# Computing one of four cross-attention score products three times in every unit

## What is computed

```python
q = (x @ Wq + bq).reshape(1, B * N, H, hd)
kv = (cond @ Wkv + bkv).reshape(1, -1, 2, H, hd)
q, k, v = _fq_sym(q, -1), _fq_sym(k, -1), _fq_sym(v, 2)
attn = softmax(einsum('bhqd,bhkd->bhqk', q, k))
attn = _fq_unsigned(attn, axis=-1)
out = einsum('bhqk,bhkd->bhqd', attn, v)
```

## Time and profile before

| | us |
|---|---|
| median of three runs (2273.24 to 2276.38) | 2275.49 |
| the profiled execution | 2284.15 |
| its span, first to last instruction | 2282.2 |
| attention within the span, 1206 to 2078 | 872 |
| TensorE busy over the span | 1910.6 (84%) |
| VectorE busy over the span | 1695.9 (74%) |
| ScalarE busy over the span | 1592.8 (70%) |

### The profile page before, as it was taken

One profiled execution on the slowest core, in us unless ns is written; L12 is line 12 of the kernel. 1 busy time (PEld: TensorE's weight loads), 2 busy tenths in 40 slices (PEclk: granted clock), 3 DMA queues, 4 the chain that ended last, 5 costly groups with the idle time before them and its releaser, 6 DMA issues. The chain is left out here.

```text
span 2282.2 us, 40123 instructions
## 1 busy us (share of the span) xinstructions
PE 1910.6 (84%) x12006; PEld 1240.5 (54%) x12006; DVE 1695.9 (74%) x2836; ACT 1592.8 (70%) x2475; POOL 525.3 (23%) x430
## 2 busy tenths in 40 slices
PE   6988999999999999997877777777777777775999
PEld 5776877777777878786552222222222222222787
DVE  5885676777777776768877888888888888885433
ACT  4667888888888888887377777777777777774211
POOL 2002555555555555554000000000000000002001
PEclk8998999999999999999895555555555555555999
DMA  4000000000000000000106888878888878886000
GB/s 131 15 5 28 0 28 0 28 0 28 0 28 0 28 12 16 28 0 25 36 1 120 156 153 153 156 150 153 154 152 153 155 151 153 155 158 143 10 10 19
DMA packets 557870, 164.78 MB, mean 72 GB/s; under 512 B 535040, under 2 KB 550272, under 8 KB 557824
## 3 DMA queue, kind: packets, MB, share of 16 engines
q1 hardware_dynamic: 557824, 164.18, 35.4%
HBM read 27.83 MB, written 2.10 MB: 13 GB/s over the span
## 5 line engine op out<-in xcount | busy, mean ns | idle before, releaser
L1247 ACT ACTIVATE levels<-s_ps,nb,qstep 128x1024 int16<-128x1024 f32 x512 | 612.2, 1199 | 235.9 <-DVE nb L1187 235.9
L1176 DVE TENSOR_REDUCE mx<-s_ps 128x1 f32<-128x512 f32 (+1 forms) x768 | 661.3, 868 | 93.6 <-PE s_ps L1122 85.6
L1122 PE MATMUL s_ps<-kT,qT 48*128 48x512 bf16 x1024 | 521.1, 611 | 233.5 <-ACT levels L1247 232.0
L602 DVE SCALAR_TENSOR_TENSOR xs<-x_ps,cw,xs 128x508 f32<-128x508 f32 (+2 forms) x393 | 291.4, 741 | 174.2 <-ACT xs L524 135.8
L1122 PEld LDWEIGHTS s_ps<-kT,qT 48*128 (+1 forms) x1024 | 82.2, 103 | 483.0 <-issue 460.9
L493 PE MATMUL o_ps<-wo,hid 128*128 x1024 | 242.9, 380 | 5.0 <-DVE acc L589 5.0
L658 POOL TENSOR_TENSOR hid<-y,sg 128x512 f32<-128x512 f32 x128 | 175.5, 1371 | 277.5 <-ACT sg L546 184.8
L1132 PEld LDWEIGHTS ao_ps<-vi,levels_T 128*128 128x128 f16 x4096 | 129.3, 105 | 185.5 <-issue 185.5
L1472 POOL MEMSET minus_half_o<- 128x4 f32 x1 | 0.1, 103 | 998.6 <-POOLq L1065 998.6
L493 PEld LDWEIGHTS o_ps<-wo,hid 128*128 128x128 f32 x1024 | 192.7, 189 | 39.5 <-issue 9.9
L524 ACT ACTIVATE xs<-x_ps,cb,cw 128x512 f32<-128x512 f32 x131 | 101.9, 777 | 116.2 <-PE x_ps L445 116.1
(11 more groups left out here) (196 smaller groups left out, 3244.8 us busy)
## 6 DMA issues: line engine op xcount, KB each, us to landing
w_raw<-winT_dram SPq DMA_DIRECT2D x18, 512.0 KB, 4.5
wo_raw<-woutT_dram SPq DMA_DIRECT2D x9, 512.0 KB, 5.8
levels_T<-levels SPq DMA_TRANSPOSE x256, 4.3
acc<-xT_dram SPq DMA_DIRECT2D x4, 512.0 KB, 6.1
w_bc<-winT_dram SPq DMA_DIRECT2D x16, 128.0 KB, 2.3
acc<-x_dram SPq DMA_DIRECT2D x1, 2048.0 KB, 11.2
att<-ctxT_dram SPq DMA_DIRECT2D x4, 512.0 KB, 6.0
out_dram<-f_out SPq DMA_DIRECT2D x16, 128.0 KB, 1.7
```

The lines of the kernel that those rows point to most:

```text
L602: dve.scalar_tensor_tensor(to, x_ps[:, :, 0:SEQ - s], cw[:, head, TAPS - 1 - s], to, ALU.mult, ALU.add).then_inc(chain if s < TAPS - 1 els ...
L1122: return pe.matmul(s_ps[:, BANKS[h % 2][chunk], :], qT[0:PARTS * HD, bass.ds(round_, 1), h % NH, :].rearrange("p b t -> p (b t)"), kT[:, h ...
L1176: dve.tensor_reduce(mx[:, h % 2, at:at + 1], src, AX.XY if what == "cd" else AX.X, ALU.max).then_inc(max_done, 1)
L1247: act.activation(levels[:, s, half * HALF:(half + 1) * HALF].rearrange("p (c k) -> p c k", c=2), s_ps[:, first:first + 2, :], ACT.Exp, bia ...
```

## The change

In `body` of TensorE, the product b of unit n+2 is issued three times instead of once. All three read the same keys and queries, write the same bank with the same values, and each starts a new sum (`start=True, stop=True`), so the scores are the same. Only the third increments `b_ready`. Nothing changes in the operands: keys and queries keep 48 rows. The products that stand ahead of the loop (units 0 and 1) stay single. So two more matmuls run in every unit but the last two, 508 in all, each with its own weight load.

```diff
                     if exists(qt, h, 2):
+                        for _ in range(2):
+                            score(qt, h + 2, "b")
                         score(qt, h + 2, "b").then_inc(b_ready, 1)
```

## The result

The changed kernel takes 2344.14 us in the median of four runs (2335.04 to 2344.63), against 2275.93 for the kernel before: 1.0292 times its time, with a 95% interval of 1.0265 to 1.0318. That is 68 us slower, where 76 us were forecast.

The account below looks back on a forecast made before the run. A ring of engine waits bounds attention, 3.32 us per unit; delaying c and d makes it 3.66. 256 x 0.34 = 87 us, less 11 at tile ends, gives +76: 2275.5 + 76 = 2352 us, range 2245 to 2385.

Parts of the forecast that it names:

- The bound: In attention no engine is full; a ring of waits between ScalarE, VectorE and TensorE sets the pace, at 3.32 us per unit.
- The two paths: Loops of waits around the engines in attention: through product a, 3.32 us per unit, and through c and d, 3.23.
- The added products delay c and d by 0.85: On TensorE, c and d queue behind the two added products; c would start 2.32 us after a instead of 1.47.
- Path A: Exponential, product a, its maximum, bias, next exponential: 3.32 us per unit, unchanged because a stands ahead of the added products.
- Path B: Two-unit loop through c, d and VectorE's wide maximum over them: 6.46 us grows to 7.31, 3.66 per unit, becoming the bound.
- The maximum over b: On VectorE: b ready 1.89 us after a's start, 0.24 late, but its maximum has slack.
- The tile ends hide 0.7 us each: VectorE's `steps` and `finish` cost 1.6 us per query tile; 0.7 would hide in its new wait, 11 us back in all.
- Weight loads cost nothing: Each added product's reload of its 48 x 128 weights runs beside the preceding product: 0; unhidden, up to 25 us more.
- The clock stays at 0.5: TensorE's clock stays low through attention although its busy share rises to 87%; low clock with path B as bound: chance 0.64.
- the first and the second rival: TensorE's clock rises and stays, 2225 us, chance 0.13; or goes up and down, 2240 to 2325 us, chance 0.13.
- Rival 3: VectorE's order has overlooked slack, so only TensorE's own time counts, 3.18 against 3.32: no change, 2276 us, chance 0.05.

## Why the prediction was right, and what was off

- *The bound.* Right. The two paths were read from one unit of the timeline, and the runs that add the same work in three places (205, 68 and 8 us) show both.
- *The added products delay c and d by 0.85.* Right: c starts 2.33 after a (2.32 forecast), the wide maximum waits 0.80.
- *Path A keeps 3.32.* Right: the shorter unit of each pair is 3.32 to 3.33. (The written-out rounds have units of 3.20 before and pairs of 7.10 after, a step of 0.35 per unit, which the sum priced like the loop's.)
- *Path B 7.31 for two units.* Too long by 0.09. The mis-sized term is the wide maximum and the one over a: I had the row with both back to back, 1.82, called it an overlap of the records and put in the sum of the single durations, 1.92. The pair measures 7.23 here, with 2.01 from the wide maximum to the bias, which is 1.82 + 0.19. The merged row was the right price. With it, the step is 0.29 us per unit instead of 0.34, and 256 x 0.29 - 11 = 63 us, which is what attention grew by. That the forecast of 76 lies only 8 from the measured 68 is in part luck: in attention it is 13 too high, and 5 us from elsewhere came on top.
- *The maximum over b.* Right: it starts 1.90 after a (1.89 forecast) and holds nothing up.
- *The tile ends hide 0.7 us each.* Right as far as the profile tells: 16 units in the loop took 58.6 us against 54.7, 3.9 more, where eight pairs of 7.22 against 6.65 would make 4.6.
- *Weight loads cost nothing.* Right: c starts where three streams of 0.427 put it.
- *The clock stays at 0.5.* Right, but it was the weakest step, and partly luck: no row told what 48 rows count for, I argued from the pauses, and gave 0.26 to cases in which it rises. The run with five products shows that in this kernel not even a TensorE without pauses raises it on 48-row products. So the first and the second rival had less chance than I gave them, since their condition, that 48 rows are taken like 128, is false.
- *Rival 3, the pause hides it.* Wrong for this order of work, and nearly right for another: with the value product behind c and d, TensorE's own pause takes up nearly all of the added work (8 us are left).

The Trainium skill, page TensorE: Matmul & The Clock Gate, section What's actually happening, tells of the clock by how busy the engine is. Here a TensorE busy for 597.88 of 600 us with 48-row products stayed at 0.50, and one busy for 364.48 us with 128-row products had 0.94. The measurements decide: busy time alone doesn't say what the clock does in this kernel.

## What to carry to other kernels

In a ring of engines, price an added instruction by what is queued behind it and whose wait ends last there: follow each path around the ring, over as many units as the buffers reach ahead, and compare their lengths; an engine's pause is no cover if the next thing in its queue is on a path. Where the profile has a row in which two instructions run back to back, use that row and not the sum of two durations. If TensorE sits at the low clock in a stage with narrow products, try rows before density: added rows of zeros cost 10 us here, all ahead of attention. Neither the rows alone nor added products alone raised the clock; both together did.

## What the hardware showed that was not expected

**The rows in use decide whether dense work raises the clock, and rows of zeros count.** With 48 rows of the contraction the clock, once down at the start of attention, never left 0.50, with TensorE busy for up to 597.88 of 600 us; with 96 rows and b three times it didn't either (527.39 us busy); with 128 rows and the same products it was 0.94. The 80 added rows of the moving operand were all zero, those of the stationary one were not; zeros on both sides were not tried. What lies between 96 and 128 rows, and whether 96 rows with more products would do, was not tried either.

**48 rows beside 128 cost TensorE time, 96 beside 128 do not.** At the low clock the value product, which uses 128 rows, starts 0.94 us after a where the scores use 48 rows, and 0.80 to 0.81 us after it where they use 128 (b once in both). Timelines of the kernel before and of the one with 128 rows and b once (PEld are weight loads):

```profile
1240.62 1.01 PE L1122 MATMUL s_ps<-kT,qT 48*128 48x512 bf16 x2 [0.70 <-ACT levels L1247]
...
1241.56 0.51 PEld L1132 LDWEIGHTS ao_ps<-vi,levels_T 128*128 128x128 f16 x16 [0.83 <-issue]
1241.56 0.60 PE L1132 MATMUL ao_ps<-vi,levels_T 128*128 128x16 f16 x16
...
1242.09 1.03 PE L1122 MATMUL s_ps<-kT,qT 48*128 48x512 bf16 x2
```

```profile
1242.20 1.01 PE L1132 MATMUL s_ps<-kT,qT 128*128 128x512 bf16 x2 [0.91 <-ACT levels L1257]
1242.58 0.15 PEld L1142 LDWEIGHTS ao_ps<-vi,levels_T 128*128 128x128 f16 x1 [0.27 <-issue]
...
1243.01 0.62 PE L1142 MATMUL ao_ps<-vi,levels_T 128*128 128x16 f16 x16
...
1243.48 1.01 PE L1132 MATMUL s_ps<-kT,qT 128*128 128x512 bf16 x2
```

From a to c it is 1.47 with 48 rows and 1.28 with 128, 0.19 less. The kernel with 96 rows and b three times changes between 96 and 128 rows as often as the first one changes between 48 and 128, and yet has the shorter time:

```profile
1242.99 1.87 PE L1133 MATMUL s_ps<-kT,qT 96*128 96x512 bf16 x4 [0.49 <-ACT levels L1260]
...
1244.22 0.15 PEld L1143 LDWEIGHTS ao_ps<-vi,levels_T 128*128 128x128 f16 x1 [0.28 <-issue]
...
1244.64 0.62 PE L1143 MATMUL ao_ps<-vi,levels_T 128*128 128x16 f16 x16
...
1245.12 2.15 PE L1133 MATMUL s_ps<-kT,qT 96*128 96x512 bf16 x4
```

From a to c it is 2.13 here, which is 1.28 and two added products of 0.427; with 48 rows and b three times it is 2.33. So it isn't the change of row count as such. What the rows do show is the first weight load of the value product: it begins 0.42 to 0.43 us ahead of that product where the scores use 96 or 128 rows, and together with it where they use 48. Why 48 rows hold that load back was not tested.

The 0.19 is the size of what the pairs of units gained without any rise of the clock: 7.02 against 7.22 with 96 rows and b three times, and 6.66 against 6.80 with 128 rows and b twice, where path A stops the gain.
